# Key stacks of attention 2 copied in two column halves, and a mask added by VectorE for two heads in the last group of attention 1

## The reference, cut to what matters

```python
# attention 1 (per batch; mask is 512 x 1601)
scores = einsum('bhqd,bhkd->bhqk', Q, K) / sqrt(16)
scores = where(mask == 0, -1e9, scores)
x = layernorm(softmax(scores) @ V @ Wo.T + bo + query) * ln_g + ln_b
# Mamba-2 block: in_proj, causal convolution, silu, a decaying state, gate, out_proj
h = x + rms(y * silu(z)) @ out_proj_w
# attention 2
q = layernorm(h) @ Wq;  k = enc @ Wk;  v = enc @ Wv
out = h + softmax(q @ k.T / sqrt(32)) @ v @ Wo
```

## Time and profile before

| | |
|---|---|
| runs | 8695.27 us median of 3 (8695.15 to 8697.0) |
| profiled execution | 8695.25 us |
| its span, first to last instruction | 8693.3 us |
| mean granted clock of TensorE | 0.927 |
| busy: TensorE, VectorE, ScalarE, GpSimd | 7601.7, 4991.8, 3399.7, 1907.4 us |

### The profile page before, as it was taken

One profiled execution on the slowest core, in us unless ns is written; L12 is line 12 of the kernel. 1 busy time (PEld: TensorE's weight loads), 2 busy tenths in 40 slices (PEclk: granted clock), 3 DMA queues, 4 the chain that ended last, 5 costly groups with the idle time before them and its releaser, 6 DMA issues.

```text
span 8693.3 us, 128104 instructions
## 1 busy us (share of the span) xinstructions
PE 7601.7 (87%) x37572; PEld 3396.5 (39%) x37572; DVE 4991.8 (57%) x12397; ACT 3399.7 (39%) x4278; POOL 1907.4 (22%) x1864
## 2 busy tenths in 40 slices
PE   3989889898998989889898898989989899898988
PEld 0343433434334343433434334343343433434343
DVE  3566465664656556465664656646566564656646
ACT  0424435243352434435244352433524335252443
POOL 3040130402203031130401304023030311303113
PEclk6989999899998989989899898999989999898998
DMA  3142240423314132131422304233141331314223
GB/s 72 26 79 37 39 69 10 79 37 50 57 21 75 30 61 55 21 69 27 76 40 36 67 14 79 37 47 60 20 76 30 56 58 19 71 30 71 45 36 61
DMA packets 216827, 422.15 MB, mean 49 GB/s; under 512 B 35673, under 2 KB 126715, under 8 KB 215945
## 3 DMA queue, kind: packets, MB, share of 16 engines
q1 hardware_dynamic: 214103, 413.20, 27.9%
q10 hardware_dynamic: 2048, 0.53, 0.0%
HBM read 191.17 MB, written 8.54 MB: 23 GB/s over the span
## 4 chain that ended last, share of the span: by engine, by line
PE 69%; DVE 11%; issue 8%; DMA 6%; ACT 3%; POOL 1%; SPq 1%; DVEq 0%; ACTq 0%; POOLq 0%
PE ps L1029 14%; PE ps L966 11%; PE ps L1000 8%; PE ps L1002 8%; PE ps L928 7%; DVE mx L1635 6%; PE ps L1004 4%; DMA kst<-khl 4%; PE ps L1034 4%; PE ps L1148 2%; PE ps L985 2%; PE ps L1239 1%; DMA qst<-q1hl 1%; PE ps L1267 1%; ACT PR L1406 1%
## 5 line engine op out<-in xcount | busy, mean ns | idle before, releaser
L1406 ACT ACTIVATE PR<-ps 128x1024 f32<-128x1024 f32 x2496 | 2499.6, 1024 | 2505.0 <-PE ps L1002 1494.4
L1606 DVE CUSTOM_DVE_ANT_0 ps<-ps,maskq 128x402 f32<-128x402 f32 x4203 | 2409.0, 587 | 1505.6 <-PE ps L966 1362.7
L1029 PE MATMUL ps<-PR,vbuf 128*32 128x512 f32 x9984 | 1343.3, 610 | 5.1 <-ACT PR L1406 5.1
L1002 PE MATMUL ps<-maskk,identb 128*128 128x512 bf16 x3328 | 1263.4, 380 | 0.0
L966 PE MATMUL ps<-kst,qst 96*128 96x402 bf16 (+1 forms) x3115 | 1019.5, 340 | 79.5 <-DVE mx L1606 64.3
L1635 DVE TENSOR_REDUCE mx<-ps 128x2 f32<-128x804 f32 x1024 | 932.6, 987 | 167.8 <-PE ps L985 164.9
L985 PE MATMUL ps<-kst,qst 100*128 100x402 f32 x2048 | 744.2, 488 | 257.8 <-DMA qst<-q1hl 155.4
L1000 PE MATMUL ps<-qst,kst 99*128 99x512 bf16 x2496 | 950.7, 381 | 0.0
L1004 PE MATMUL ps<-qst,kst 102*128 102x512 f32 x1664 | 767.9, 525 | 100.2 <-ACT PR L1406 70.8
L966 PEld LDWEIGHTS ps<-kst,qst 96*128 96x128 bf16 x3115 | 281.8, 97 | 1182.3 <-DVE mx L1606 821.3
L746 POOL MEMSET kst<- 96x252 f32 (+1 forms) x34 | 8.7, 255 | 3063.1 <-PE ps L1029 3016.6
(11 more groups left out here) (197 smaller groups left out, 7669.8 us busy)
## 6 DMA issues: line engine op xcount, KB each, us to landing
kst<-khl SPq DMA_DIRECT2D x96, 800.5 KB, 16.1
kst<-khl SPq DMA_DIRECT2D x300, 200.1 KB, 7.4
stage<-in_maskt SPq DMA_DIRECT2D x204, 256.0 KB
stage<-in_mask SPq DMA_DIRECT2D x204, 201.0 KB
ctxs<-in_ctxt SPq DMA_DIRECT2D x17, 1601.0 KB, 25.8
qst<-q1hl SPq DMA_DIRECT2D x96, 256.0 KB
win_s<-in_w_in SPq DMA_DIRECT2D x16, 1288.0 KB, 5.7
KS<-khl SPq DMA_DIRECT2D x102, 200.1 KB
```

The costliest lines, as they stand in the source:

```text
L1002: mm = pe.matmul(o, identb[:, :], maskk[:, t, :], start=False, stop=True)
L1029: mm = pe.matmul(ps[32 * j:32 * j + 32, 6, :], l, PR[:, t % 2, j, :], start=(t == 0), stop=(t == KT - 1), tile_position=(0, 32 * j))
L1406: nc.scalar.activation(PR[:, t % 2, 2 * half:2 * half + 2, :], ps[:, 2 * half:2 * half + 2, :], ACT.Exp, scale=scale).then_inc(s_p, 1)
L1606: nc.vector.tensor_tensor_reduce(src, src, maskq[:, i, c0:c0 + w], 1.0, -3.0e38, ALU.add, ALU.max, mx[:, c, h * QT + i:h * QT + i + 1]).th ...
```

## The change

**Key stacks in halves.** `KHALF` cuts the 1601 columns after two chunks: 804 and 797 columns. `stack_k1` now copies one half: it waits for the two chunks of that half alone and issues three copies of about 400 KB. There is a semaphore for each group and half. In `take`, chunks 0 and 1 of block 1 wait for the first half of `KS1[0]`, and chunks 2 and 3 for the second. TensorE's row maxima wait for both.

**The mask in the last group.** In group `G0 - 1` half 1 no longer has its two mask matmuls. VectorE waits for the half's scores (`s_s`), adds `maskk[:, t, :]`, repeated for both heads, to 128 x 1024 PSUM elements in place, and signals `s_mk`; ScalarE's exponential of that half waits for `s_mk`. The sum has the same terms, with the mask in bf16 as before.

```diff
-        s_k1 = [sem(f"s_k1_{g}") for g in range(G1)]
+        s_k1 = [[sem(f"s_k1_{g}_{e}") for e in range(2)] for g in range(G1)]
+        KHALF = [(0, KCH[NC // 2][0]), (KCH[NC // 2][0], S)]
...
-            def stack_k1(b, g):
-                sp.wait_ge(s_restfree, rests(b, K1[NC * (g + 1) - 1]) + 1)
+            def stack_k1(b, g, half):
+
+                sp.wait_ge(s_restfree, rests(b, K1[NC * g + NC // 2 * (half + 1) - 1]) + 1)
                 alone(sp)
+                lo, hi = KHALF[half]
                 for n, (kpart, qpart) in enumerate(TERMS1):
-                    sp.dma_start(f(KS1[g][HD1 * n:HD1 * (n + 1), :, 0:S]), f(khl1[:, kpart, 0:S])).then_inc(s_k1[g], 16)
+                    sp.dma_start(f(KS1[g][HD1 * n:HD1 * (n + 1), :, lo:hi]), f(khl1[:, kpart, lo:hi]))\
+                        .then_inc(s_k1[g][half], 16)
...
                 for g in range(G1):
-                    stack_k1(b, g)
+                    for half in range(2):
+                        stack_k1(b, g, half)
...
                         if gi < G0:
-                            pe.matmul(o, KS[gi][0:SROWS, h, t * P:(t + 1) * P], QS[gi][0:SROWS, h, :],
-                                      start=True, stop=False)
-                            mm = pe.matmul(o, identb[:, :], maskk[:, t, :], start=False, stop=True)
+                            added = gi == G0 - 1 and half == 1
+                            mm = pe.matmul(o, KS[gi][0:SROWS, h, t * P:(t + 1) * P], QS[gi][0:SROWS, h, :],
+                                           start=True, stop=added)
+                            if not added:
+                                mm = pe.matmul(o, identb[:, :], maskk[:, t, :], start=False, stop=True)
...
-                            act.wait_ge(s_k1[0], LEAD + (b + 1) * STACK1)
+                            act.wait_ge(s_k1[0][i[1] // (NC // 2)], LEAD + (b + 1) * STACK1)
...
                     for half in range(2):
+                        if gi == G0 - 1 and half == 1:
+                            act.wait_ge(s_mk, b * KT + t + 1)
                         act.wait_ge(s_s, b * 2 * NG * KT + (gi * KT + t) * 2 + half + 1)
...
                 for t in range(KT + 1):
+                    if gi == G0 - 1 and t < KT:
+                        dve.wait_ge(s_s, b * 2 * NG * KT + (gi * KT + t + 1) * 2)
+                        nc.vector.tensor_tensor(ps[:, 2:4, :], ps[:, 2:4, :],
+                                                maskk[:, t, :].unsqueeze(1).broadcast_to([P, 2, T]), ALU.add)\
+                            .then_inc(s_mk, 1)
```

More of the change, by code:

```diff
@@ L289, in xattn_mamba @@
         s_p = sem("s_p")
+        s_mk = sem("s_mk")
         s_pv = sem("s_pv")
@@ L580, in stack_q1 @@
                     sp.dma_start(f(QS1[g][HD1 * n:HD1 * (n + 1), :, :]), f(q1hl[:, g, qpart, :])).then_inc(s_qs1[g], 16)
-            for first in (*s_stack, *s_mload, *s_k1, *s_qs1, *s_mload1, s_out):
+            for first in (*s_stack, *s_mload, *s_k1[0], *s_k1[1], *s_qs1, *s_mload1, s_out):
                 sp.nop(nofuse=True).then_inc(first, LEAD)
@@ L973, in entry1 @@
                 if kind == "raw" and k == 0:
-                    pe.wait_ge(s_k1[g], LEAD + (b + 1) * STACK1)
+                    for half in range(2):
+                        pe.wait_ge(s_k1[g][half], LEAD + (b + 1) * STACK1)
                     pe.wait_ge(s_k1pad, G1 * (b + 2))
@@ L1354, in take @@
                             for g in range(G1):
-                                act.wait_ge(s_k1[g], LEAD + b * STACK1)
+                                for half in range(2):
+                                    act.wait_ge(s_k1[g][half], LEAD + b * STACK1)
                         dst, bias = khl[:, 0, c:c + w], bk_c[:, i[0]:i[0] + 1]
```

## The result

The changed kernel takes **8669.0 us** (median of 8 runs, 8662.72 to 8673.09); the kernel before took 8695.21 in the same comparison (8 runs, 8693.4 to 8697.32). The ratio is 0.9968 with a 95% interval of 0.9958 to 0.9979: faster by 26 us, where 147 were forecast. The profiled execution took 8669.73 us with a span of 8668.0, and TensorE's mean granted clock was 0.922, where it had been 0.927.

What follows compares the result with a forecast made beforehand. TensorE was taken as the bound, busy for 87% of the span. Halves gain 13.15 us and the mask costs 3.9, so 9.2 us for each of 16 batches, 147 us: 8695 to 8548 us, range 8490 to 8630.

Steps and rivals of the forecast that it cites:

- Halves, 13.15 us a batch: Key projections: copying the key stacks in halves removes ScalarE's wait and TensorE's idle time, a gain of 13.15 us a batch.
- Rivals 2 and 3: Key stacks: a half costs nearly a whole copy, 8805 us, chance 0.04; second half somewhat late, 8575 to 8620 us, 0.06.
- Mask, +3.9 us a batch: Last group of attention 1: moving two mask matmuls a tile to VectorE costs 3.9 us a batch, bounds 2.5 to 7.
- The ring: Last group, half 1: matmul, VectorE, ScalarE and back to TensorE in series take 3.09 us a tile, more than 2.85.
- VectorE's step 1.23: Last group, half 1: VectorE's mask addition over 1,024 PSUM columns takes 1.23 us, between bounds of 1.2 and 1.4.
- the last half to its value product 3.0: End of the last group: from the start of the last half 1 to its value product, 3.0 us instead of 2.2.
- Rival 1: Last group: TensorE stays the bound, so the mask's part gains; 17.6 us a batch in all, 8413 us, chance 0.05.
- Rival 4, the clock: Last group: TensorE's clock falls because it idles 0.7 us in every tile; net +9 us a batch, 8840 us, chance 0.05.
- the 21 us a batch: Last group: cost if the clock fell to 1.2 GHz, 4.8 us a tile, 1.95 us more over 11 intervals.
- the end at +0.8 us: End of the last group: the last value product comes 0.8 us later, part of the mask's cost.
- The step that failed: Slow-clock stretches elsewhere in an iteration: left out of the sum, allowed 3 us a batch either way, about 50 us.

Runs made afterwards that it cites:

- mask_one_head: The changed kernel, but in the last group VectorE adds the mask to head 2 alone while TensorE does head 3's mask: 8532.51 us, ratio 0.981.
- one_head_each_half: The changed kernel, but in the last group VectorE adds the mask for one head of each half and TensorE for the other: 8477.71 us, ratio 0.9747.
- 1: One part at a time: the changed kernel with the mask matmuls back on TensorE, 8574.36 us; the kernel before with only the mask addition on VectorE, 8816.27 us.
- 2: The changed kernel with one useless matmul at the scan's first chunk, where TensorE waits for VectorE: 8683.8 us, ratio 0.9984.
- 3: `halves_only` with one or three useless fp32 matmuls of 512 columns ahead of the scan: 8581.84 us and 8589.7 us.
- 5: `mask_one_head`, 8532.51 us; from the last group's end to the iteration's end its instructions are those of `halves_only`.
- 4: The changed kernel with nine useless bf16 matmuls, six ahead of the last group's last value product and three after it: 8638.59 us, ratio 0.9931.
- halves_only: The changed kernel with the last group's mask matmuls back on TensorE, so key stacks in halves alone: 8574.36 us, ratio 0.9854.

## Why the prediction was wrong

Time: 8669 against a forecast of 8548 and a range from 8490 to 8630; the sign was right, the size was not.

- *Halves, 13.15 us a batch*: right as the size of that stretch. It lost 12.88 us, the distance of the projection chunks is 4.94 where 4.78 was said, and both halves were in time, by over 6 us where about 5 were said. Rivals 2 and 3 are out. The rate of the smaller copies hardly fell: 118 GB/s at 1006 to 1008, while the second half's copies are under way, beside 122 for the 800 KB ones; from the first issue to the last landing block 0 took 22.9 us in halves and 23.7 whole. One reading of the prediction is wrong: the clock did not fall at the end of TensorE's idle time but near 1014.7, about halfway through it. The Trainium skill's advice to batch (DMA: Bandwidth & Descriptors, "Bandwidth") would have had them clearly slower; no run here shows that for these copies.
- *Mask, +3.9 us a batch*: right, +3.60. The ring gave 3.09 us a tile, measured 3.07; VectorE's step 1.23, measured 1.232 (mean of 208; with 0.70 for half the columns in `mask_one_head` that leaves 0.17 us that does not scale, as was assumed); the last half to its value product 3.0, measured 3.06 (955.77 to 958.83). Rival 1 is out for this edit; `one_head_each_half` comes near it.
- *Rival 4, the clock*: wrong in its place, right in its kind. Within the tiles the clock stays at 1.00, in every iteration from 2 to 15, though TensorE is busy for 8.42 us of 10:

```profile
930.00:940.00 10.00, 8.42 (x45) 1.87 (x44) 3.74 (x4) 6.46 (x7) 0.00 (x0) 1.00 0.01 2
```

  So the 21 us a batch did not come. The Trainium skill's rule on small idle times between groups of matmuls through PSUM (TensorE: Matmul & The Clock Gate, "A second HAM failure mode: psum-queue depth-cycling") would have had it oscillate there; this trace doesn't agree. It falls at the group's end instead, where 1.46 and 0.72 us of idle time lie close together, for 1.95 us a batch. The prediction had the end at +0.8 us and asked nothing of the clock behind it.
- *The step that failed* is the one left out of the sum: "the stretches at the slow clock elsewhere in an iteration may move, appear or go", with 3 us a batch allowed either way, from four matmuls at 1.9 us. The stretches that neither edit touches lost **7.5 us a batch**, all of it one way: 1.95 behind the last group, 3.56 in the scan and 0.93 in the row maxima, 6.4 together and all with more low clock than before, and 1.03 in attention 2 and the next group 0, which the clock does not explain. The size failed because I took one batch of four matmuls as the unit, while in the scan alone 8.3 us more at the low clock cost 3.56 us, since there the chain goes to and fro between TensorE and VectorE and nothing hides it. And the sign was not even. I had booked as gain the low-clock work that went with the stall (2.7 of the 13.15 us). It did go from there (13.2 to 3.2 us a batch at 1.2 GHz), but the total at 1.2 GHz rose from 1270 to 1352 us.

Shown: the low clock in the scan needs no mask edit (1) and is not contention (1, 2); the same instructions run at either clock in different iterations of one execution (3), and in two versions that differ ahead of them alone (5); the fall behind the last group is made by the mask's idle time (4). Not shown: why, that is, what decides at which of the light places the clock falls. In 5 both the moment and TensorE's load ahead of the scan differ, so that it does not separate the two; the unequal iterations in 3 speak for the moment. The versions with fillers moved the stretches, and none of them took them away; I can't forecast from these runs which shift would.

## What to carry to other kernels

When an edit removes a stall, do not count the whole stretch as gained: with the halves alone TensorE no longer stood for 10.44 us a batch, and the kernel gained 7.7. Set a term for the clock against it: go through the light places that follow, and price a low stretch at each by what lies on the chain there. All nine versions here gave time back and none gained by it; that the kernel before sat at a lucky offset is a guess. When a step moves to another engine, put it where a half of the work is under way anyway. The same two mask matmuls cost 3.6 us a batch when both heads of one half wait for VectorE, and gain 4.0 when one head of each half does.

## What the runs showed that I had not expected

- Iterations of one execution have a few lengths, not a spread: the changed kernel alternates irregularly between about 525.8 and 528.9 us (scan 46.4 and row maxima 59.95, or 47.8 and 61.9), while the kernel before stays at 529.1 (528.6 to 529.5).
- Useless matmuls behind which nobody waits can make a kernel faster: nine bf16 ones in each batch took 30 us off the changed kernel. Three fp32 ones in a place on the chain of `halves_only` added 15 us.
- VectorE's addition in place in PSUM costs nearly what it does in the other memory: 1.232 us for 1,024 columns, beside 1.216, and 0.70 us for 512.
